# Order of two products in one PSUM accumulation: the second bias layer first, its correction products last

## Chip, core and metric

One Trainium2 chip, one of its cores, one launch. The metric is the device time of the launch in microseconds (us), lower is better. The engines are named as in the profile: PE is the matrix engine (PEld its weight loads), DVE the vector engine, ACT the scalar engine, POOL GpSimd, SP the engine that issues the DMAs.

## The reference, cut to what matters

Two layers of a deformable attention block run on x of shape (2, 128, 32, 32): 2 layers x 2 images, called four segments. Each has 8 heads of 16 channels, 1024 queries and 64 sampled keys. Most of the work is the position bias, a small network that is evaluated for each pair of query and key:

```python
pos = grid_q[:, :, None, :] - grid_kv[:, None, :, :]          # 1024 x 64 pairs, x and y, for each head
bias = jnp.sign(pos) * jnp.log1p(jnp.abs(pos))
bias = jax.nn.relu(bias @ cpb_w1 + cpb_b1)                    # 2 -> 32
bias = jax.nn.relu(bias @ cpb_w2 + cpb_b2)                    # 32 -> 32, the second layer
bias = (bias @ cpb_w3 + cpb_b3).reshape(b, GROUPS, H * W, Hd * Wd)   # 32 -> 1
sim = jnp.einsum('bhid,bhjd->bhij', qh, kh) + bias
attn = jax.nn.softmax(sim, axis=-1)
```

Before it come a grouped 1x1 product (q), a strided depthwise convolution, gelu, tanh, and a bilinear sampling of the image; after it the weighted sum of values, an output product with residual, and an MLP of 128 -> 512 -> 128 with residual.

## The kernel before, in words

The bias network is cut into 256 steps g: 4 segments x 4 pairs of heads (a pair of heads is a unit) x 16 steps. A step handles 16 keys and half of the queries (512): `ROWS` = 4 groups of 32 partitions and `CT` = 4 groups of 32 columns. Eight steps make a phase. In a step:

- DVE, `first_layer` (L565), writes h1, the first layer. It computes max(hx, hy') in one 128x2048 instruction, with hx = w1x*fx + b1 and hy' = -w1y*fy. Since relu(a + b) = max(a, -b) + b, what is stored lacks a term that depends on y alone. Three h1 buffers (`H1_BUFS`) let DVE run ahead; buffer g is free when pair 2(g-3)+1 is filled.
- PE, `layer2` (L753 to L774), sums in four PSUM banks (two "pairs" z(2g) and z(2g+1) of 1024 columns) the two parts of the second layer: the **correction products** (L766), sixteen matmuls of 32 partitions x 32 columns of bf16 weights `u_rows` against `fy`, which bring w2 times the missing term and the bias b2; and the **w2 products** (L771), sixteen matmuls of the same tile size in fp32, each of which the chip runs as two instructions. Ahead of the correction products of row groups 0 and 2 stands `turn`, the wait for the pair to be empty; between the two kinds stands the wait for h1.
- ACT, `relu2` (L426), reads each filled pair in one 128x1024 instruction and writes h2; the ring has three pairs (`RING`), so z(2g+1) of a step takes the pair that z(2g-2), the first pair of the step before, had.
- PE, `layer3` (L783), for the step before: four fp32 matmuls of 128 x 32 onto `scores`.

Other stages are put behind the step's own work by a table of slots (`BEFORE_SLOTS`, `AFTER_SLOTS`, `SOFTMAX_SLOTS`): PE runs `layer2(g)`, then `scores_start` (L795, once a phase), `layer3(g-1)`, then what the table names. In every phase slot 1 has the transposes (L873) and slot 2 the products that take off the maximum (L880). Slots 28 to 50 of a segment prepare the next one: among them on DVE `norm1`, `conv_products`, `hats` (L662) and `hat_products` (L668), on PE `q` (L818), `spread` (L842) and `sample` (L854). Slots 3 to 24 finish the segment before with `exp_sums`, `attend` (L891), `project` (L905), four `mlp_up` (L914) and `mlp_down` (L924). SP issues the loads of `fy` of a unit (`load_fy`) once the last z of the unit two before is filled, and `load_features` (hx, hy) when its h1 have been made; both serve a unit that starts 16 steps later.

Of the kernel before, what the change touches and what calls it, by code (L numbers as in the profile page):

```python
# [15 lines left out]
LAYERS, B, C, H, W = 2, 2, 128, 32, 32  # L16
# [18 lines left out]
ROWS = CT = 4  # L35
# [8 lines left out]
H1_BUFS = H2_BUFS = 3  # L44
# [128 lines left out]
def build(nc, x_in, consts, weights, x_out, features_dram, fy_dram, reciprocals_dram):  # L173
    with ExitStack() as ctx:
        def sb(name, shape, dt=F32):
            return ctx.enter_context(nc.sbuf_tensor(name, shape, dt))
# [4 lines left out]
        def sem(name):  # L181
            return ctx.enter_context(nc.semaphore(name))
# [35 lines left out]
        h1 = [sb(f"h1_{k}", [128, CT, HALF]) for k in range(H1_BUFS)]  # L218
# [5 lines left out]
        u_rows = [sb(f"u_rows{l}", [128, 128], BF16) for l in range(LAYERS)]  # L224
# [35 lines left out]
        h1_ready = sem("h1_ready")  # L260
# [15 lines left out]
        def w(l, name):  # L276
            a, b = COLS[name]
            return wts[l][:, a:b]
# [5 lines left out]
        def bank(h):  # L284
            return slice(HALF * h, HALF * (h + 1))

        def pair_of(stage, n):
            return pairs[PLACE[stage, n][0]]
# [461 lines left out]
        def _(pe):  # L750
            def layer2(g):


                unit, h, t = g // UNIT_STEPS, g // STRIDES % 2, g % STRIDES
                l = unit // PAIRS // B
                if g % UNIT_STEPS == 0:
                    pe.wait_ge(fy_loaded[unit % 2], 16 * ROWS * (unit // 2 + 1))
                    pe.wait_ge(u_ready, l + 1)
                z = [pair_of("z", 2 * g + r // 2)[:, bank(r % 2)] for r in range(ROWS)]
                key = [slice(32 * r, 32 * (r + 1)) for r in range(ROWS)]  # L760
                for r in range(ROWS):
                    if r % 2 == 0:
                        turn("z", 2 * g + r // 2)
                    y = fy[unit % 2][key[r], t, H // 2 * h:H // 2 * (h + 1)]
                    for c in range(CT):
                        pe.matmul(z[r][32 * c:32 * (c + 1)], u_rows[l][key[r], 32 * c:32 * (c + 1)],  # L766
                                  y.unsqueeze(2).broadcast_to([32, H // 2, W]), start=True, stop=False)
                pe.wait_ge(h1_ready, g + 1)
                for r in range(ROWS):
                    for c in range(CT):  # L770
                        ins = pe.matmul(z[r][32 * c:32 * (c + 1)], w(l, "w2")[key[r], key[r]], h1[g % H1_BUFS][key[r], c],  # L771
                                        start=False, stop=True)
                    if r % 2:
                        filled("z", 2 * g + r // 2, ins)  # L774

# [23 lines left out]
            def turn(stage, n):  # L799
                pair, _, before, _ = PLACE[stage, n]  # L800
                if before:
                    pe.wait_ge(pair_emptied[pair], before)

            def filled(stage, n, ins):
                ins.then_inc(pair_filled[PLACE[stage, n][0]], 1)
# [130 lines left out]
            for g in range(LAST_STEP + 1):  # L936
                if g == SEG_STEPS // 2:
                    pe.wait_ge(early_loaded[1], 16)
                    pe.wait_ge(late_loaded[1], 16)
                if g < ALL_STEPS:  # L940
                    layer2(g)
                if 1 <= g <= ALL_STEPS:
                    if g % STRIDES == 1:
                        scores_start(g // STRIDES)
                    layer3(g - 1)
                for name, n in PLAN["pe"].get(g, []):
                    stages[name](n)
# [92 lines left out]
```

## Time and profile before

| | |
|---|---|
| Time, three runs | 929.76 us median (927.41 to 930.80) |
| The profiled execution: its own time | 930.51 us |
| its span, first to last instruction | 928.7 us |
| mean granted PE clock | 0.97 of full speed |
| PE, DVE, ACT busy, share of the span | 91%, 77%, 69% |
| the 256 steps | 49.4 to 880 us of the span |
| a phase with nothing but its own stages | 22.41 us |

The profiled execution's own time is 1.8 us above its span, and 0.75 us above the median of the three runs. The span is one execution's; matmul durations in it are start to modelled end, and matmuls on different tiles overlap, so what a group costs PE is read from its start to the start of the group behind it.

### The profile page before, as it was taken

Reading aid. Unit: us, or ns where it says so; the run is one execution under the profiler, and the core shown is the slowest. Engines: PE = TensorE matmul, PEld = TensorE weight load, DVE = VectorE, ACT = ScalarE, POOL = GpSimd, SP = SyncE. Lnnn points to the kernel's source line nnn. Section 1 sums busy time; section 2 is a strip of 40 time slices with the busy share of each in tenths; the row PEclk is TensorE's granted clock in tenths of the full one; section 3 lists DMA queues with packets and bytes.
Section 4 is the critical chain, followed back from the end, with each engine's and each line's share of the span. In section 5 each row is a group of like instructions: output and inputs, shape, how many; then the busy total and the mean of one; then the engine's idle time right before and its main releaser. Section 6 shows DMA issues by size and latency. Waiting matters only on the chain.

```text
span 928.7 us, 34427 instructions
## 1 busy us (share of the span) xinstructions
PE 848.8 (91%) x15908; PEld 300.5 (32%) x15908; DVE 713.9 (77%) x472; ACT 639.5 (69%) x717; POOL 59.9 (6%) x40
## 2 busy tenths in 40 slices
PE   2179999989999999989999999999999999999936
PEld 1123323333333333323333333323333333333312
DVE  3678799898878659998878849989887749888411
ACT  1347768867777858877776857896777757777711
POOL 2200002120000002040000002040000000000000
PEclk9589999999999999999999999999999999999978
DMA  4210101011101101002011101002011101000010
GB/s 146 59 52 3 50 2 50 7 49 13 51 10 41 28 2 49 8 14 48 26 28 27 50 1 50 9 2 57 5 51 27 50 1 43 11 3 3 2 48 23
DMA packets 29535, 27.89 MB, mean 30 GB/s; under 512 B 22096, under 2 KB 24016, under 8 KB 29392
## 3 DMA queue, kind: packets, MB, share of 16 engines
q1 hardware_dynamic: 29392, 25.69, 10.6%
q8 instruction: 126, 2.06, 0.9%
q14 instruction: 17, 0.14, 0.1%
HBM read 23.05 MB, written 2.49 MB: 27 GB/s over the span
## 4 chain that ended last, share of the span: by engine, by line
PE 83%; DVE 8%; ACT 3%; DMA 3%; issue 2%; SPq 0%; POOL 0%; ACTq 0%; POOLq 0%; DVEq 0%
PE pair L771 29%; PE scores L783 24%; PE pair L766 9%; PE scores L795 3%; PE pair L914 3%; PE scores L880 3%; DVE h L565 3%; PE pair L924 3%; PE pair L873 2%; ACT h L426 2%; DVE big L668 2%; PE pair L891 1%; PE pair L905 1%; PE pair L818 1%; PE pair L854 1%
## 5 line engine op out<-in xcount | busy, mean ns | idle before, releaser
L426 ACT ACTIVATE h<-pair 128x1024 f32<-128x1024 f32 x512 | 496.5, 1022 | 201.9 <-PE pair L771 201.6
L565 DVE TENSOR_TENSOR h<-hx,hy 128x2048 f32<-128x2048 f32 x256 | 579.9, 2300 | 41.4 <-PE pair L771 41.1
L771 PE MATMUL pair<-h,wts 32*32 32x512 f32 x8192 | 346.6, 597 | 9.7 <-DVE h L565 9.7
L783 PE MATMUL scores<-h,wts 128*32 128x512 f32 x2048 | 273.6, 606 | 0.9 <-ACT h L426 0.9
L771 PEld LDWEIGHTS pair<-h,wts 32*32 32x32 f32 x8192 | 135.2, 103 | 29.3 <-DVE h L565 13.5
L766 PE MATMUL pair<-fy,u_rows 32*32 32x512 bf16 x4096 | 118.7, 386 | 27.4 <-DMA fy<-fy_dram 20.1
L783 PEld LDWEIGHTS scores<-h,wts 128*32 128x32 f32 x2048 | 43.6, 108 | 209.2 <-issue 208.4
L766 PEld LDWEIGHTS pair<-fy,u_rows 32*32 32x32 bf16 x4096 | 37.6, 88 | 196.7 <-issue 178.4
L691 DVE TENSOR_REDUCE neg_max<-pair 128x8 f32<-128x512 f32 x32 | 22.1, 691 | 70.3 <-PE pair L873 70.3
L306 POOL TENSOR_TENSOR conv_prod<-qpad,wts 128x288 f32<-128x288 f32 x16 | 21.6, 1379 | 440.3 <-ACT qpad L452 440.3
L406 POOL TENSOR_TENSOR big<-big,hat_x 128x512 f32<-128x512 f32 x16 | 35.5, 2248 | 119.0 <-DVE big L662 119.0
L719 DVE SCALAR_TENSOR_TENSOR x<-pair,wts,x 128x1024 f32<-128x1024 f32 x4 | 5.1, 1284 | 42.2 <-PE pair L924 42.2
L518 ACT ACTIVATE big<-pair,wts 128x1024 f32<-128x1024 f32 x16 | 17.8, 1114 | 27.7 <-PE pair L914 27.7
L880 PEld LDWEIGHTS scores<-const,neg_max 128*64 128x64 f32 x512 | 27.3, 136 | 27.0 <-issue 23.5
L880 PE MATMUL scores<-const,neg_max 128*64 128x128 f32 x512 | 35.0, 279 | 0.8 <-DVE neg_max L691 0.8
L914 PE MATMUL pair<-work,wts 128*128 128x512 f32 x64 | 32.7, 643 | 2.2 <-DVE work L713 2.2
L795 PE MATMUL scores<-qpad,keys_t 128*32 128x512 f32 x256 | 34.1, 605 | 0.0
L924 PE MATMUL pair<-big,wts 128*128 128x512 f32 x64 | 28.5, 598 | 1.3 <-ACT big L518 1.3
L512 ACT ACTIVATE probs<-scores,wts 128x512 f32<-128x512 f32 x32 | 22.0, 687 | 8.2 <-PE scores L880 8.0
L435 ACT ACTIVATE probs<-scores,wts 128x512 f32<-128x512 f32 x32 | 22.1, 692 | 1.3 <-PE scores L783 1.3
L873 PEld LDWEIGHTS pair<-const,probs 128*128 128x128 f32 x128 | 13.4, 140 | 27.7 <-issue 26.0
L873 PE MATMUL pair<-const,probs 128*128 128x128 f32 x128 | 21.0, 287 | 0.8 <-ACT probs L435 0.8
(87 smaller groups left out, 342.6 us busy)
## 6 DMA issues: line engine op xcount, KB each, us to landing
hx<-features_dram SPq DMA_DIRECT2D x64, 128.0 KB, 2.7
hy<-features_dram SPq DMA_DIRECT2D x64, 128.0 KB, 3.1
att_den<-reciprocals_dram SPq DMA_DIRECT2D x4, 512.0 KB
wts<-weights_dram SPq DMA_DIRECT2D x2, 960.0 KB, 8.5
fy_dram<-fy_part SPq DMA_DIRECT2D x96, 8.0 KB, 1.5
x<-x_dram SPq DMA_DIRECT2D x2, 512.0 KB, 5.9
fy<-fy_dram SPq DMA_DIRECT2D x64, 12.0 KB
out_dram<-x SPq DMA_DIRECT2D x2, 512.0 KB, 4.9
```

Source lines behind the costliest of these rows:

```text
L406: pool.tensor_tensor(bilinear[:, k], hat_y[:, k], hat_x[:], ALU.mult).then_inc(bilinear_ready[0], 1)
L426: emptied("z", 2 * g + j, act.activation(h2[g % H2_BUFS][:, 2 * j:2 * (j + 1)].rearrange("p r n -> p (r n)"), pair_of("z", 2 * g + j)[:], ...
L435: act.activation(probs[:, unit % PAIRS, bank(h)], scores[phase % 2][:], ACT.Identity, bias=w(seg // B, "b3"))\
L565: dve.tensor_tensor(h1[g % H1_BUFS][:].rearrange("p c (y x) -> p c y x", x=W), hx[unit % 2][:, :, t].unsqueeze(2).broadcast_to([128, CT, H ...
L766: pe.matmul(z[r][32 * c:32 * (c + 1)], u_rows[l][key[r], 32 * c:32 * (c + 1)], y.unsqueeze(2).broadcast_to([32, H // 2, W]), start=True, s ...
L771: ins = pe.matmul(z[r][32 * c:32 * (c + 1)], w(l, "w2")[key[r], key[r]], h1[g % H1_BUFS][key[r], c], start=False, stop=True)
L783: ins = pe.matmul(scores[phase % 2][32 * r:32 * (r + 1)], w(l, "w3")[:, 32 * t:32 * (t + 1)], h2[g % H2_BUFS][:, r], start=False, stop=t = ...
L795: pe.matmul(scores[phase % 2][k], keys_t[seg % 2][:, u, k], qpad[seg % 2][:, 1 + H // 2 * h:1 + H // 2 * (h + 1), 1:W + 1], start=True, st ...
L873: ins = pe.transpose(pair_of("scores_t", phase)[:, s], probs[:, unit % PAIRS, bank(h)][:, s], cst("ident"))
L880: ins = pe.matmul(scores[phase % 2][NKV * n:NKV * (n + 1), 128 * k:128 * (k + 1)], neg_max[phase % 2][:, 2 * k + n:2 * k + n + 1].broadcas ...
L914: ins = pe.matmul(pair_of("mlp_up", n)[:, bank(h)], w(seg // B, "mlp_w1")[:, 128 * c:128 * (c + 1)], xn2[:, bank(h)], start=True, stop=True)
L924: ins = pe.matmul(pair_of("mlp_down", seg)[:, bank(h)], w(seg // B, "mlp_w2")[:, 128 * c:128 * (c + 1)], mlp_h[:, c, bank(h)], start=c == ...
```

## The change

In `layer2` the two kinds of product change places. The w2 products come first and start each PSUM accumulation; the correction products come second, end it, and the last one of each pair signals that the pair is filled. `turn` (the pair is empty) and the wait for h1 now both stand ahead of the w2 products; the waits for `fy` and `u_rows`, once a unit, stand between the two kinds. The instructions, their number, shapes and data are the same.

```diff
                 unit, h, t = g // UNIT_STEPS, g // STRIDES % 2, g % STRIDES
                 l = unit // PAIRS // B
+                z = [pair_of("z", 2 * g + r // 2)[:, bank(r % 2)] for r in range(ROWS)]
+                key = [slice(32 * r, 32 * (r + 1)) for r in range(ROWS)]
+                pe.wait_ge(h1_ready, g + 1)
+                for r in range(ROWS):
+                    if r % 2 == 0:
+                        turn("z", 2 * g + r // 2)
+                    for c in range(CT):
+                        pe.matmul(z[r][32 * c:32 * (c + 1)], w(l, "w2")[key[r], key[r]], h1[g % H1_BUFS][key[r], c],
+                                  start=True, stop=False)
                 if g % UNIT_STEPS == 0:
                     pe.wait_ge(fy_loaded[unit % 2], 16 * ROWS * (unit // 2 + 1))
                     pe.wait_ge(u_ready, l + 1)
-                z = [pair_of("z", 2 * g + r // 2)[:, bank(r % 2)] for r in range(ROWS)]
-                key = [slice(32 * r, 32 * (r + 1)) for r in range(ROWS)]
                 for r in range(ROWS):
-                    if r % 2 == 0:
-                        turn("z", 2 * g + r // 2)
                     y = fy[unit % 2][key[r], t, H // 2 * h:H // 2 * (h + 1)]
                     for c in range(CT):
-                        pe.matmul(z[r][32 * c:32 * (c + 1)], u_rows[l][key[r], 32 * c:32 * (c + 1)],
-                                  y.unsqueeze(2).broadcast_to([32, H // 2, W]), start=True, stop=False)
-                pe.wait_ge(h1_ready, g + 1)
-                for r in range(ROWS):
-                    for c in range(CT):
-                        ins = pe.matmul(z[r][32 * c:32 * (c + 1)], w(l, "w2")[key[r], key[r]], h1[g % H1_BUFS][key[r], c],
-                                        start=False, stop=True)
+                        ins = pe.matmul(z[r][32 * c:32 * (c + 1)], u_rows[l][key[r], 32 * c:32 * (c + 1)],
+                                        y.unsqueeze(2).broadcast_to([32, H // 2, W]), start=False, stop=True)
                     if r % 2:
                         filled("z", 2 * g + r // 2, ins)
```

## Rows read from the trace of the kernel before

**Rows 1.** The page: busy time, and the chain that ended last.

```profile
PE 848.8 (91%) x15908; PEld 300.5 (32%) x15908; DVE 713.9 (77%) x472; ACT 639.5 (69%) x717; POOL 59.9 (6%) x40
PE 83%; DVE 8%; ACT 3%; DMA 3%; issue 2%; SPq 0%; POOL 0%; ACTq 0%; POOLq 0%; DVEq 0%
```

**Rows 2.** Timeline of PE in a plain phase: start, us, group.

```profile
812.15 0.43 PE L766 MATMUL pair<-fy,u_rows 32*32 32x512 bf16 x16
812.37 1.34 PE L771 MATMUL pair<-h,wts 32*32 32x512 f32 x32
813.64 1.07 PE L783 MATMUL scores<-h,wts 128*32 128x512 f32 x8
814.64 0.43 PE L766 MATMUL pair<-fy,u_rows 32*32 32x512 bf16 x16
814.87 1.34 PE L771 MATMUL pair<-h,wts 32*32 32x512 f32 x32
...
816.04 1.94 ACT L426 ACTIVATE h<-pair 128x1024 f32<-128x1024 f32 x2
```

**Rows 3.** Busy time in four phases of eight steps: length, PE, PEld, DVE, ACT, POOL, clock, DMA.

```profile
812.15:834.56 22.41, 22.41 (x480) 7.57 (x477) 19.57 (x12) 16.75 (x19) 0.00 (x0) 1.00 0.01 2
...
339.12:364.70 25.58, 25.58 (x493) 9.14 (x490) 24.44 (x17) 19.99 (x22) 5.90 (x4) 1.00 0.17 44
364.70:391.34 26.64, 24.75 (x500) 9.68 (x496) 25.70 (x25) 23.65 (x30) 0.00 (x0) 1.00 0.05 9
391.34:419.79 28.45, 25.70 (x544) 9.06 (x541) 26.16 (x18) 22.77 (x27) 9.45 (x4) 1.00 0.09 24
```

**Rows 4.** The waits of the whole span: us in total, times, longest.

```profile
ACT h L426 <- PE pair L771: 201.6, 197, 17.4
DVE h L565 <- PE pair L771: 41.1, 55, 2.1
PE pair L771 <- DVE h L565: 9.7, 12, 1.6
```

**Rows 5.** L771 alone in short stretches: matmuls, loads that ran or had run (x).

```profile
814.86:814.96 0.10, 0.09 (x8) 0.10 (x9) 1.00 0.00 0
...
57.82:57.84 0.02, 0.02 (x16) 0.02 (x28) 1.00 0.00 0
...
58.21:58.22 0.01, 0.01 (x24) 0.00 (x0) 1.00 0.00 0
```

**Rows 6.** Timeline: loads issued behind the correction products' start, stretch cut at 841.2 us.

```profile
840.99 0.43 PE L766 MATMUL pair<-fy,u_rows 32*32 32x512 bf16 x16
841.05 0.18 PEld L771 LDWEIGHTS pair<-h,wts 32*32 32x32 f32 x9
```

**Rows 7.** Timeline, the steps at 57.7 us and at 199.1 us.

```profile
57.71 1.15 PE L771 MATMUL pair<-h,wts 32*32 32x512 f32 x32 [1.12 <-DVE h L565]
58.79 1.07 PE L795 MATMUL scores<-qpad,keys_t 128*32 128x512 f32 x8
...
58.91 1.02 ACT L426 ACTIVATE h<-pair 128x1024 f32<-128x1024 f32 x1 [1.20 <-PE pair L771]
...
199.11 1.15 PE L771 MATMUL pair<-h,wts 32*32 32x512 f32 x32 [0.73 <-DVE h L565]
```

**Rows 8.** The line L766: duration ns min/median/max of its matmuls.

```profile
L766 PE MATMUL pair<-fy,u_rows x4096: 384/385/605, 49.4 to 876.9; 32*32 32x512 bf16 x196
```

**Rows 9.** Timeline of the start: the wait for fy, then for the first h1.

```profile
49.43 0.66 PE L766 MATMUL pair<-fy,u_rows 32*32 32x512 bf16 x16 [20.08 <-DMA fy<-fy_dram]
50.54 2.02 PE L771 MATMUL pair<-h,wts 32*32 32x512 f32 x32 [0.45 <-DVE h L565]
```

**Rows 10.** Behind a wait for h1: timeline; then two stretches, clock eighth column.

```profile
118.60 2.02 PE L771 MATMUL pair<-h,wts 32*32 32x512 f32 x32 [1.65 <-DVE h L565]
...
118.60:122.20 3.60, 3.60 (x40) 0.49 (x40) 3.60 (x2) 1.63 (x2) 0.00 (x0) 0.53 0.00 0
...
173.40:176.80 3.40, 3.40 (x58) 0.92 (x56) 2.29 (x1) 3.01 (x4) 0.00 (x0) 0.51 0.00 0
```

## Prediction

> **What bounds the kernel now.** I read the page first: PE is busy 91% of the span and the chain that ended last lies 83% on it [rows 1], so what the change does to PE's own sequence comes first. Then the timeline of PE in a phase that has no other work than its own. There a step takes 814.64 - 812.15 = 2.49 us, without a gap: 0.22 us from the correction products to the w2 products, 1.27 us from these to layer 3, and 1.00 us from layer 3 to the next step [rows 2]. PE is the bound in such a phase; DVE is busy 19.57 of 22.41 us [rows 3]. The waits say the same: PE waited for h1 only 12 times, 9.7 us in all, while ACT waited for PE 197 times and DVE 55 times [rows 4]. The exception is the three phases in which DVE prepares the next segment: DVE busy is 24.44 of 25.58, 25.70 of 26.64 and 26.16 of 28.45 us [rows 3]. Three of the four segments have such a stretch.
>
> **The change, step by step.** No instruction, byte or DMA is added. What moves is where the w2 products stand, and the trace of before happens to show them both ways.
>
> 1. *w2 products behind correction products (now).* The reader should see that the 1.27 us are not what sixteen tiles need. The first instruction of each fp32 product starts on eight tiles together; the other eight have not started 0.1 us later, and nine loads are in (the first of [rows 5]). In the next view too exactly nine w2 loads get in while the correction products hold the tiles [rows 6]. The second half of the tiles starts late, and everything behind it on those tiles too.
>
> 2. *w2 products on tiles that are free (the other order's case).* At 57.71 us PE had waited for h1, the correction products were long through, and the same 32 instructions took 58.79 - 57.71 = 1.08 us to the start of the next group [rows 7]. All sixteen first instructions ran within 0.12 us (the second of [rows 5]). So 1.27 - 1.08 = 0.19 us a step is a cost of standing behind the bf16 products. After the change they stand behind layer 3, whose tiles have another size; a group behind such a switch starts with no load done ahead (L795 stands so too and starts at once [rows 7]). I take it as the free case.
>
> 3. *Correction products behind w2 products (new).* The trace has no row of it. Lower bound: their loads go in while the second fp32 instructions run, and they add only what they now take up to the next start, 0.22 us [rows 2]: 1.08 + 0.22 = 1.30 us against 1.49 now. Upper bound: no load gets in until the w2 matmuls have ended (1.15 us after their start [rows 7]), then a load of about 0.1 us (0.18 us for nine overlapped loads in rows 6 is the nearest row), then the products (0.43 us to their end, of which some 0.1 overlaps the next group [rows 2]): about 1.15 + 0.1 + 0.3 = 1.55, that is 0.06 us more than now. I take the lower one, because in rows 6 loads do go in under running matmuls of the same tiles, from the moment these have started.
> A rule bears on this. The Trainium skill ("TensorE: Matmul & The Clock Gate", Part 3) says that a weight load overlaps matmuls in flight only when the row group differs; by it the upper bound would hold and the step would not shrink. The trace disagrees with the rule as worded: the w2 loads start 0.06 us after the correction matmuls of the same row groups, which take 0.385 us each [rows 6, 8]. That page's Part 2 adds the background weight buffer, which would fit.
>
> 4. *The ACT loop, which is next late.* z(2g+1) takes the pair that relu reads first in the step before, and the wait for it now stands ahead of the w2 products of row group 2 instead of ahead of the short products. Counted from the w2 products' start: eight second instructions have started at 0.50 (58.21 [rows 5]), one lasts about 0.43 on its tile (the step from first to second, 57.71 to 58.16), so the last correction product of row group 1 starts at 0.93; it lasts 0.385 [rows 8]; ACT starts some 0.12 behind an end (58.91 against 58.21 + 0.59) and takes 1.02 [rows 7]: 2.46, and a wake-up of 0.05 (estimate) makes 2.51. Row group 2 wants the pair 0.06 after the start of the next w2 products, so nothing stalls in a step of 2.45 us or more; with 1.30 + 1.00 = 2.30 us a step it comes 0.15 late. A late step is longer, which gives the next one its time back, so steps would alternate between 2.30 and 2.45: 0.075 lost on the average. Now the same count leaves the pair empty at 0.22 + 1.17 + 1.02 + 0.05 = 2.46 after the step's start, some 0.06 before it is wanted at 2.49 + 0.03 [rows 2, 7], so that the loop hardly shows.
>
> 5. *The h1 loop.* h1 is wanted 0.22 us earlier in a step and given back 0.22 us later. With three buffers and 2.3 to 2.5 us a step DVE keeps some 3 us in hand, and in a plain phase 22.41 - 19.57 = 2.8 us of it are idle [rows 3]. No cost there. In the three stretches DVE has nothing to spare, and what PE saves PE then waits.
>
> 6. *Waits for fy and u.* The waits on fy move behind the w2 products. Only the first is ever long (20.08 us), and there h1 comes later still, at 50.54 [rows 9]. Now the correction products of step 0 run in that wait; after, they stand behind the w2 products at half clock: +0.4 us. The loads of SP stay where they were, a unit ahead; what releases them (the last z) comes at the same place of the step.
>
> **The sum.** 256 steps. 72 lie in the three stretches, 184 outside; of these 3 already start free (of the 12 waits nine lie in the stretches, three in each like the one at 199.11 us, and three before and outside them [rows 4, 7]), so 181 x 0.19 = 34.4 us. Of the 23 phases outside, six steps in eight follow a step with no other stage, 138, less 8 in each of three segments that follow a stage of slots 3 to 22: 114 x 0.075 = 8.6 us back to the ACT loop. The stretches: a phase can't be shorter than DVE's busy time plus the 0.95 us that the tightest has (26.64 - 25.70), which leaves 0.2 us in one phase of a stretch and little more in the first segment: 2 us in all. The start: -0.4. Together 34.4 - 8.6 + 2 - 0.4 = 27.4 us. The profiled execution took 930.51 us, hence 903.1; it is 0.75 above the median of the runs, which I leave in the rounding: 903 us.
>
> **Rivals.**
> - *No gate by ACT.* If the pair is free in time after all, 8.6 us come back, and if the stretches gain half of 63 x 0.19 instead of 2 us, 4 more: about 890 us. For it: ACT is only 75% busy in a phase [rows 3]. Against: the count of step 4.
> - *The loads of the correction products don't go in early* (the upper bound of step 3). Then a step has 2.55 instead of 2.49 us: 184 x 0.06 = +11 us, 941 us. It decides from the point where the correction products start more than about 1.18 us after the w2 products (0.99 by my count). For it: no row shows bf16 behind fp32 on the same tiles. Against: rows 6. With only the streaming waited for, the start would be at 1.08 and the step 2.4: no ACT gate, 915 us.
> - *DVE is the bound everywhere.* If DVE's lead fails at each unit's `hidden_terms` and each phase's `score_max`, a phase would stay near 22 instead of about 21.3: some 0.4 x 23 = 9 us gained, 920 us. Against: 2.8 us of idle DVE a phase.
> - *The clock.* Behind a wait of PE for h1 the clock was granted at 0.53 for 3.60 us, the 1.2 GHz level [rows 10], some 1.8 us lost; a second such dip at 173.4 us lies in the first stretch, in which PE also waits. Longer waits in the stretches may add one or two for each: +4 to +10 us on top of any case.
>
> **How the numbers follow.** Chances: forecast with its own range 896 to 913: 0.5; no ACT gate, 884 to 896: 0.14; a gain cut to a few us by DVE or by partly hidden loads, 913 to 925: 0.18; no change: 0.06; loads not hidden, or dips that eat the gain: 0.12. Below 884 I leave 0.04 of the second, above 926 the last two, so the range 884 to 926 leaves out about 0.2. 0.5% of the time is 4.6 us, about what a measurement of this kernel tells from no change. Faster by more than that: 0.82; within: 0.06; slower: 0.12.
>
> **What the profile of the changed kernel would show.** In a plain phase the w2 matmuls take 1.08 to 1.3 us of start to last end with all sixteen tiles started in 0.12 us, the correction products start some 0.9 to 1.0 us after them, and layer 3 1.30 us after them (step 3 wrong if 1.4 or more). Steps alternate near 2.30 and 2.45, and the second half of the w2 products shows a wait for L426 (step 4 wrong if steps are all 2.30). A plain phase lasts 21.2 to 21.4 us. The stretches keep their length within 1 us, with more waits for L565. More than two mid-run stretches of low clock would spoil the sum. PE's busy time drops by about what the span does, DVE's and ACT's stay.

## The result, and the profile after

| | before | after |
|---|---|---|
| Time, median of 13 runs each on the same chip | 930.49 us (927.41 to 931.77) | 934.37 us (930.23 to 938.0) |
| Ratio, with its 95% interval | | 1.0044 (1.003 to 1.0057) |
| Profiled execution: own time, span | 930.51, 928.7 us | 934.73, 932.9 us |
| Mean granted PE clock | 0.97 | 0.967 |

The change made the kernel 3.9 us slower, within the half per cent that was called no change; 903 us had been forecast, with a range to 926. In the kernel after, L763 are the w2 products and L771 the correction products; layer 3 is still L783.

The page of the kernel after and the longest wait for PE in it, against [rows 1, 4] (a wait: us in total, times, longest):

```profile
PE 850.2 (91%) x15908; PEld 314.9 (34%) x15908; DVE 715.4 (77%) x472; ACT 639.9 (69%) x717; POOL 59.9 (6%) x40
```

```profile
ACT h L426 <- PE pair L771: 210.2, 194, 17.9
```

PE is busy 91% of the span as before, ACT waits for it as often, and the counts of instructions are equal. The answer lies inside a step. Timeline of the kernel after, a plain step (start, us, group, idle before), against [rows 2]:

```profile
828.81 1.21 PE L763 MATMUL pair<-h,wts 32*32 32x512 f32 x32
829.26 0.28 PEld L771 LDWEIGHTS pair<-fy,u_rows 32*32 32x32 bf16 x2 [0.15 <-issue]
829.69 0.68 PE L771 MATMUL pair<-fy,u_rows 32*32 32x512 bf16 x16
829.88 0.20 PEld L771 LDWEIGHTS pair<-fy,u_rows 32*32 32x32 bf16 x14 [0.34 <-issue]
...
830.30 1.06 PE L783 MATMUL scores<-h,wts 128*32 128x512 f32 x8
...
831.30 0.66 PE L763 MATMUL pair<-h,wts 32*32 32x512 f32 x8
```

From w2 to the correction products it is 829.69 - 828.81 = 0.88 us, from these to layer 3 0.61, from layer 3 to the next step 1.00: 2.49 us, as before. The w2 products now have the free case's early second halves, as forecast. But the correction products, which took 0.22 us when they stood first, take 0.61 now. Two of their loads go in ahead; the other fourteen come from 829.88 on, 0.19 us after the first product has started. L771 alone shows it (us, PE busy (x), PEld busy (x), clock):

```profile
829.75:829.76 0.01, 0.01 (x1) 0.00 (x0) 1.00 0.00 0
829.98:829.99 0.01, 0.01 (x15) 0.01 (x12) 1.00 0.00 0
```

One correction product is under way 0.06 us after the first, and 0.29 us after it there are fifteen. In [rows 5] it was the w2 products that had only eight tiles going while their ninth load was in. The lag has moved from one set to the other: 1.49 us from a step's start to layer 3, as before.

Plain phases are equal to 0.01 us (842.76 - 820.36 = 22.40, [rows 3] 22.41). The 3.9 to 4.2 us lie elsewhere, and the starts of L795, once a phase, show where. The kernel after is behind by 1.78 us at the first, 2.55 at the second, 1.27 at the fourth (130.06 against 128.79), 1.98 after the first stretch (212.32 against 210.34), 2.61 after the second (427.46 against 424.85), 4.31 after the third and 4.20 at the last. Three things make up these steps.

*The start*, timelines against [rows 7, 9]:

```profile
49.76 2.02 PE L763 MATMUL pair<-h,wts 32*32 32x512 f32 x32 [21.30 <-issue]
52.33 3.42 PE L854 MATMUL pair<-big,image_t 128*32 128x128 f32 x64
...
58.38 1.74 PE L763 MATMUL pair<-h,wts 32*32 32x512 f32 x32 [1.49 <-DVE h L565]
60.57 1.08 PE L795 MATMUL scores<-qpad,keys_t 128*32 128x512 f32 x4
```

Before, the correction products of steps 0 and 1 ran while PE waited for h1. Now PE idles there, and they come behind. In step 0 it is 2.57 us from w2 to the sampling products L854 (49.76 to 52.33), against 1.95 before (50.54 to 52.49); h1 came 0.78 us earlier in this execution, which hid these 0.62 us. But the clock stayed at the 1.2 GHz level until 55.4 us (0.50 from 53.9 to 55.4, where the kernel before had 1.00), and from L854 to the products behind it, L864, it took 3.85 us against 3.02. That is why step 1 starts 0.67 us later. In step 1 it takes 2.19 us from w2 to L795 against 1.08. Behind an awaited h1 at full clock it is 1.50 (see below), so 0.42 us of this comes with the order, and the other 0.69 with the 1.2 GHz level, which begins at 58.8 us. Together 0.67 + 1.11 = 1.78.

*The stretches.* A late h1, the kernel after, against the 199.11 us of [rows 7]:

```profile
200.69 1.15 PE L763 MATMUL pair<-h,wts 32*32 32x512 f32 x32 [0.85 <-DVE h L565]
201.57 0.68 PE L771 MATMUL pair<-fy,u_rows 32*32 32x512 bf16 x16
202.19 1.06 PE L783 MATMUL scores<-h,wts 128*32 128x512 f32 x8
```

Behind an awaited h1 stand 1.50 us instead of 1.08. Phases inside the stretches (length, PE, PEld, DVE, ACT, POOL, clock). The kernel before, the second phase of the first and of the second stretch:

```profile
182.91:210.34 27.43, 25.02 (x544) 9.01 (x541) 26.40 (x18) 20.36 (x25) 8.85 (x4) 1.00 0.17 42
396.35:424.85 28.50, 26.03 (x544) 9.10 (x541) 27.48 (x18) 20.60 (x25) 8.85 (x4) 1.00 0.16 41
```

The kernel after, the second phase of the first stretch, the first phase of the third, and a short piece at low clock:

```profile
184.29:212.32 28.03, 25.12 (x548) 9.68 (x540) 27.17 (x18) 20.41 (x24) 9.05 (x4) 1.00 0.18 42
585.74:614.56 28.82, 26.70 (x504) 10.01 (x496) 25.25 (x26) 25.29 (x33) 0.40 (x1) 0.94 0.04 7
389.90:393.30 3.40, 3.40 (x52) 0.73 (x42) 2.29 (x1) 3.16 (x4) 0.00 (x0) 0.50 0.00 0
```

28.03 - 27.43 = 0.60 us are lost in such a phase at full clock, and as much in the third stretch (28.05 against 27.43). In the second the kernel after is 0.47 us faster (28.03 against 28.50), but only because this execution of the kernel before lost 1.07 us in a single step: from w2 to layer 3 it took 2.34 us (420.02 to 422.36) instead of 1.27. No run says why; e7, with the same order there, has 27.42 us in this phase.

*The clock.* The last row is a stretch at the 1.2 GHz level. Between 56 and 880 us the kernel after has three more, at 58.8, 174.9 (clock 0.50 each) and 604.9 us (0.51). Before there were two, at 118.6 and 173.4 us [rows 10]. The phase at 585.74 holds the one at 604.9: 28.82 us, against 27.66 for the same phase before at clock 1.00. The missing one at 118.6 us gives 1.2 us back (the lag falls from 2.49 to 1.27).

Added up over the phases (an estimate from the differences above), the order itself costs some 2.2 us, 0.4 at the start and 0.6 in each stretch. Differences in clock cost some 3 us more, and the late step of the kernel before takes 1.1 off.

### The profile page after: what moved, and what is told of

It reads as the page before. It is cut to its first block, busy times and chain, and to the rows that moved or that the text cites. A ratio compares the mean times of both kernels' runs of the same rounds, so it can differ in the third digit from the quotient of the medians.

```text
span 932.9 us, 34682 instructions
## 1 busy us (share of the span) xinstructions
PE 850.2 (91%) x15908; PEld 314.9 (34%) x15908; DVE 715.4 (77%) x472; ACT 639.9 (69%) x717; POOL 59.9 (6%) x40
## 3 DMA queue, kind: packets, MB, share of 16 engines
HBM read 23.05 MB, written 2.49 MB: 27 GB/s over the span
## 4 chain that ended last, share of the span: by engine, by line
PE 85%; DVE 7%; issue 4%; DMA 2%; ACT 1%; POOL 0%; SPq 0%; ACTq 0%; POOLq 0%; DVEq 0%
PE pair L763 29%; PE scores L783 25%; PE pair L771 10%; PE scores L795 4%; PE pair L914 3%; PE scores L880 3%; PE pair L924 3%; DVE h L565 3%; PE pair L873 2%; PE pair L891 1%; PE pair L842 1%; PE pair L818 1%; PE pair L905 1%; PE pair L854 1%; DVE big L668 1%
## 5 line engine op out<-in xcount | busy, mean ns | idle before, releaser
L763 PE MATMUL pair<-h,wts 32*32 32x512 f32 x8192 | 313.8, 607 | 40.0 <-issue 21.3
L783 PE MATMUL scores<-h,wts 128*32 128x512 f32 x2048 | 274.5, 608 | 1.1 <-ACT h L426 1.1
L771 PE MATMUL pair<-fy,u_rows 32*32 32x512 bf16 x4096 | 180.0, 383 | 0.0
L771 PEld LDWEIGHTS pair<-fy,u_rows 32*32 32x32 bf16 x4096 | 96.2, 88 | 156.2 <-issue 120.4
L763 PEld LDWEIGHTS pair<-h,wts 32*32 32x32 f32 x8192 | 71.8, 103 | 212.5 <-issue 142.0
L783 PEld LDWEIGHTS scores<-h,wts 128*32 128x32 f32 x2048 | 43.6, 108 | 76.0 <-issue 76.0
L306 POOL TENSOR_TENSOR conv_prod<-qpad,wts 128x288 f32<-128x288 f32 x16 | 21.6, 1381 | 441.3 <-ACT qpad L452 441.3
L795 PE MATMUL scores<-qpad,keys_t 128*32 128x512 f32 x256 | 34.9, 618 | 0.0
```

The costliest lines, as they stand in the source:

```text
L771: ins = pe.matmul(z[r][32 * c:32 * (c + 1)], u_rows[l][key[r], 32 * c:32 * (c + 1)], y.unsqueeze(2).broadcast_to([32, H // 2, W]), start=F ...
L783: ins = pe.matmul(scores[phase % 2][32 * r:32 * (r + 1)], w(l, "w3")[:, 32 * t:32 * (t + 1)], h2[g % H2_BUFS][:, r], start=False, stop=t = ...
L795: pe.matmul(scores[phase % 2][k], keys_t[seg % 2][:, u, k], qpad[seg % 2][:, 1 + H // 2 * h:1 + H // 2 * (h + 1), 1:W + 1], start=True, st ...
```

## Experiments

The kernels below have the product order as a list, `ORDER(g)`, for each step: `w` is the four fp32 w2 products of a row group, `f` its four 32x32 correction products, `F` one 32x128 correction product for the whole row group in place of the four. The other lines of the edits, which only make this list work, are left out. In the timelines w2 products are L789 to L791, narrow correction products L792 to L794, wide ones L786 to L788, layer 3 L812 to L814.

**e1: w2 products alone.** Is the free case 1.08 us in every step, and does ACT gate a shorter one?

```diff
-    w0 w1 w2 w3 f0 f1 f2 f3
+    w0 w1 w2 w3                  # the waits for fy and u stay
```

> The sixteen correction products are left out (their waits are kept); the w2 products stand alone between two groups of 128x32 tiles. Three theories of the 0.19 us that the forecast lost. A, queue: behind a group that waits for busy tiles of the same tile size, PE has only part of the rest at hand and the rest starts about 0.185 us late; a change of tile size (a drain) cures it. B, type: going from bf16 to fp32 on a tile, or back, costs 0.19 us. C, throughput: sixteen tiles simply need 1.49 us for both kinds, of which 0.22 are the corrections'. A and B: the w2 products take 1.08 us from their start to layer 3's, all sixteen tiles started within 0.12 us; PE then needs 2.08 us a step, so DVE (2.27) or the ACT loop sets steps of 2.25 to 2.35 us and the time is about 870 to 885 us. C: 1.27 us from w2 to layer 3 and steps of 2.27 us at least, with the eight late tiles still there.

Measured: 864.34 us (before 929.77). Timeline of e1:

```profile
747.73 1.16 PE L789 MATMUL pair<-h,wts 32*32 32x512 f32 x32
748.82 1.06 PE L812 MATMUL scores<-h,wts 128*32 128x512 f32 x8
749.82 1.28 PE L789 MATMUL pair<-h,wts 32*32 32x512 f32 x32
751.02 1.07 PE L812 MATMUL scores<-h,wts 128*32 128x512 f32 x8
```

1.09 us to layer 3, then 1.20: steps alternate between 2.09 and 2.20. The time is below the 870 to 885 us expected, and so are the steps (2.25 to 2.35). Steps 2 and 4 of the prediction hold as mechanisms. The free case is there in a plain step. In every other step the second pair is late: in the step at 749.82 us its first w2 product starts at 750.00, 0.05 us behind the end of ACT's relu of the first pair of the step before (749.95). The correction set costs 65 us in the original order, 0.25 us a step, though its instructions are among the shortest.

**e2 and e3: the corrections as four wide products, first or last.** If the lag belongs to a second set on the same busy 32x32 tiles, a change of tile size should remove it.

```diff
-    w0 w1 w2 w3 f0 f1 f2 f3
+    F0 F1 F2 F3 w0 w1 w2 w3      # e2
+    w0 w1 w2 w3 F0 F1 F2 F3      # e3
```

> The correction products come first again, but as four matmuls of 32 partitions x 128 columns (u_rows of a row group in one weight load) instead of sixteen of 32x32; the same sums. The tile size now changes between them and the w2 products. A: corrections 0.31 us to the w2 start, then w2 in 1.08 us on free tiles: 1.39 us instead of 1.49; the rest of the step 1.00. Without another limit 2.39 us a step and about 908 us; if the wait of the second pair for ACT's relu of the step before binds at about 2.45 us, only about 920 us. B: w2 behind a change of type still takes 1.27 us: 1.58 us for both, step 2.57 us, about 948 us. C: 1.49 to 1.58, no gain.

> The changed order with the corrections as four matmuls of 32x128. A: w2 starts free (1.08 us to the corrections' start, drain included), corrections 0.31 us: 1.39 us; the gate by ACT then shows, since the pair is filled later (about 1.6 us after the w2 start): steps of 2.39 to 2.6, on average near 2.45 to 2.49; time 915 to 930 us, not better than the wide corrections first. B: 1.58 us for both, about 950 us.

Measured: e2 936.73 us, ratio 1.0072 (1.0057 to 1.0087); e3 930.42 us, 0.9999 (0.9987 to 1.0012). Timeline of e2, a step behind other stages, then a plain one:

```profile
822.31 0.40 PE L786 MATMUL pair<-fy,u_rows 32*128 32x512 bf16 x4
822.63 1.14 PE L789 MATMUL pair<-h,wts 32*32 32x512 f32 x32
...
828.15 0.57 PE L786 MATMUL pair<-fy,u_rows 32*128 32x512 bf16 x4
828.66 1.14 PE L789 MATMUL pair<-h,wts 32*32 32x512 f32 x32
829.73 1.08 PE L812 MATMUL scores<-h,wts 128*32 128x512 f32 x8
830.74 0.39 PE L786 MATMUL pair<-fy,u_rows 32*128 32x512 bf16 x2
```

Timeline of e3, the same two kinds of step:

```profile
821.97 1.14 PE L789 MATMUL pair<-h,wts 32*32 32x512 f32 x32
823.05 0.40 PE L786 MATMUL pair<-fy,u_rows 32*128 32x512 bf16 x4
823.37 1.06 PE L812 MATMUL scores<-h,wts 128*32 128x512 f32 x8
824.37 1.28 PE L789 MATMUL pair<-h,wts 32*32 32x512 f32 x32
825.58 0.40 PE L786 MATMUL pair<-fy,u_rows 32*128 32x512 bf16 x4
825.90 0.64 PE L812 MATMUL scores<-h,wts 128*32 128x512 f32 x4
```

Where nothing else holds it, the wide set costs 0.32 us in either place and w2 keeps its 1.07 or 1.08 (821.97 to 823.05): 1.39 or 1.40 us to layer 3 instead of 1.49, and the lag is gone. A plain step is 2.59 us in e2 (830.74 - 828.15) and 2.53 in e3 (825.90 - 823.37) all the same. In e2 the wide set is stretched to 0.51, in e3 the w2 set to 1.21: both are held by the pair that ACT has not emptied (in e3 the relu ends at 824.50 and the second pair's w2 products start at 824.55). What the tiles give is taken by the next loop. So the part of theory A on the tiles came as expected, but its times did not, 908 to 920 us for e2 and 915 to 930 for e3, since the wait for ACT bound at 2.59 and 2.53 us instead of near 2.45.

**e4: the kinds mixed**, so that only eight products of a second set follow at a time.

```diff
-    w0 w1 w2 w3 f0 f1 f2 f3
+    f0 f1 w2 w3 w0 w1 f2 f3
```

> Same instructions as before, another order: corrections of row groups 0 and 1, w2 of 2 and 3, w2 of 0 and 1, corrections of 2 and 3. A: the w2 products of 2 and 3 start at once on free tiles, those of 0 and 1 are the only ones to wait (0.21 us), and a group of eight that waits can be followed late by at most the eight corrections: 1.25 to 1.45 us for all instead of 1.49, time 905 to 930 us. B: each tile still changes type once within the step: 1.49, no change. C: no change.

Measured: 947.21 us, ratio 1.0189 (1.0172 to 1.0206). In its timeline the step at 817.01 us has 0.22 us to w2 (817.23), 0.86 from there to the second half of the corrections (818.09) and 0.56 to layer 3 (818.65), 1.64 us in all; in the next, w2 comes after 0.07 us and layer 3 after 1.49 (819.65 to 821.14). At best the mixed order equals the others, and it adds 0.15 us in other steps. There the w2 products of the second pair come first, and that pair is empty late: they start 0.14 us behind the end of ACT's relu in both steps (817.09 and 819.58; not tested by itself). The expectation of 905 to 930 us under theory A was missed, and this order doesn't hide the lag either.

**e5: the w2 products twice.** Is it the meeting of bf16 and fp32, or any second set on the same tiles?

```diff
-    w0 w1 w2 w3 f0 f1 f2 f3
+    w0 w1 w2 w3 w0 w1 w2 w3
```

> The correction products are replaced by the w2 products a second time (another sum): fp32 behind fp32 on the same sixteen tiles. Queue theory: the second set is late like any set behind busy tiles, both together take 0.86 + 1.04 + the late start of 0.19, about 2.1 us to the next group, and its first instructions start in two lots 0.185 us apart. Type theory: no change of type, so both take 1.08 + 0.86 = 1.94 us, all started within 0.12 us. Time about 930 + 256 x 0.5 = 1060 us at most, not the point.

Measured: 1114.68 us. Timeline of e5:

```profile
901.36 2.35 PE L789 MATMUL pair<-h,wts 32*32 32x512 f32 x64
903.64 0.64 PE L812 MATMUL scores<-h,wts 128*32 128x512 f32 x4
```

And its line L789 alone in two short stretches:

```profile
902.26:902.42 0.16, 0.16 (x17) 0.09 (x1) 1.00 0.00 0
902.50:902.51 0.01, 0.01 (x7) 0.01 (x8) 1.00 0.00 0
```

2.28 us for both sets, where two times the time to the next start (0.88, and 1.08 at the end) would be 1.96. In the 0.16 us from 902.26 on, one single load goes in; only then do the others follow. The second set's first product starts at 902.24 and the next at 902.44, the same 0.19 us; the other products then start 17 ns apart instead of 7, which is the rest of the 0.32 us (2.1 us had been expected for both sets). One type, and a first product that is alone for 0.19 us: a change of type is out as its cause.

**e6: the correction products twice, behind w2.** Is the 0.61 us a fee of the set, or one paid once?

```diff
-    w0 w1 w2 w3 f0 f1 f2 f3
+    w0 w1 w2 w3 f0 f1 f2 f3 f0 f1 f2 f3
```

> The changed order with the correction products twice (another sum): w2, corrections, corrections. The first set should start 0.88 us after w2 with a spread of 0.30 us as in the changed kernel. The second is bf16 behind bf16. Queue theory: the second set is late as well or is issued at the pace of 8 ns a tile that the first has: it adds 0.2 to 0.4 us. Type theory: it adds 0.21 us, started within 0.05 us of its turn, since the type stays.

Measured: 980.97 us. Timeline of e6:

```profile
856.24 1.21 PE L789 MATMUL pair<-h,wts 32*32 32x512 f32 x32
857.12 0.90 PE L792 MATMUL pair<-fy,u_rows 32*32 32x512 bf16 x32
857.31 0.33 PEld L792 LDWEIGHTS pair<-fy,u_rows 32*32 32x32 bf16 x30 [0.34 <-issue]
857.95 0.64 PE L812 MATMUL scores<-h,wts 128*32 128x512 f32 x4
```

Both sets together take 0.83 us; the second adds 0.22, the price that the corrections had in the original order. So sixteen bf16 products behind bf16 products cost 0.22 us even on busy tiles: behind the first two, the other thirty loads go in without a stop, and no product of the second set starts alone. That is what the type theory had expected of this run, and the low end of what the queue theory had. And the 0.39 us more is paid once, where the first of them meets the w2 products: 0.20 of it is the rest of w2's own 1.08 us (they begin at 0.88), and 0.19 is lag.

**e7: the original order where the change loses.** Steps 0 and 1 and slots 24 to 51 of the first three segments have the original order, all others the changed one.

```diff
+    if g < 2 or g < SEG_STEPS * (SEGS - 1) and 24 <= g % SEG_STEPS < 52:
+        return f0 f1 f2 f3 w0 w1 w2 w3
     w0 w1 w2 w3 f0 f1 f2 f3
```

> The changed order everywhere but in steps 0 and 1 and in slots 24 to 51 of the first three segments, where the order of before is kept (86 of 256 steps). My account now: in plain phases both orders take 22.41 us, and all of the loss is in these places: the corrections of step 0 and 1 no longer run while PE waits for h1 at the 1.2 GHz level, and behind a wait of 2.2 us for h1 near 390 and 605 us the clock drops where it did not. So this kernel should be within 0.15% of the one before, about 930 us, with low clock near 174 us at most. Rival: the loss comes from the order in all steps (a later fill of the pairs for ACT, h1 given back later); then two thirds of it stay, 933 us.

Measured: 931.55 us, ratio 1.0021 (1.0008 to 1.0033). Long stretches of e7, against 638.30 to 860.97 us of before (222.67 us long, x4362) and 860.97 to the end (67.73 us, PE 44.70 of it, clock 0.87):

```profile
638.56:861.18 222.62, 222.62 (x4361) 80.06 (x4356) 178.82 (x95) 163.11 (x177) 0.00 (x0) 1.00 0.09 21
861.18:931.10 69.92, 46.88 (x477) 17.59 (x468) 15.48 (x11) 23.45 (x25) 0.00 (x0) 0.85 0.07 24
```

The start and the stretches have their old lengths (183.02 to 210.45 us is 27.43 again), and at 861 us e7 is 0.2 us behind the kernel before instead of 4.2. The medians give back less: e7 is 2.0 us above the kernel before (931.55 against 929.58), where the change was 3.9. That lies between the two accounts (at most 0.15%, or two thirds of the loss, which is 0.29%), and an interval from 0.08% to 0.33% doesn't tell them apart. What this execution still loses, 2.2 us, lies in the last 70 us, most of it behind the last step, at a clock of 0.85 against 0.87; whether the others of its runs lose theirs there too, no profile shows. e7 also has a stretch at the 1.2 GHz level (clock 0.50 from 388.2 to 391.4 us), in steps with the original order, and is 1.3 us behind at the end of that phase. In the next the distance falls back to 0.2, but only because the kernel before has its late step there. So part of e7's closeness at 861 us is luck, and the place of such a stretch does not hang on the order of the products around it alone.

**e8: wide corrections where ACT has time.** From e2 and e3: wide products first, but only in the steps behind which another stage gives ACT its time.

```diff
+    if PLAN["pe"].get(g):
+        return F0 F1 F2 F3 w0 w1 w2 w3
     f0 f1 f2 f3 w0 w1 w2 w3
```

> The order of before, with the corrections as four matmuls of 32x128 in those steps behind which PE has another stage to run (some 110 of 256), as sixteen of 32x32 elsewhere. If the tile drain saves 0.10 us a step and only the wait for ACT's relu of the step before took it back in the kernel with wide corrections everywhere, then the stage behind gives ACT the time, and 110 x 0.10 less those in which DVE sets the pace is 6 to 10 us: 920 to 925 us. Rival: the later fill of the first pair delays ACT in the next step as well, and nothing or less than 2 us is gained.

Measured: 924.01 us, ratio 0.9932 (0.9915 to 0.9949): faster than both kernels. Timeline of e8:

```profile
790.19 0.39 PE L788 MATMUL pair<-fy,u_rows 32*128 32x512 bf16 x4
790.52 1.14 PE L791 MATMUL pair<-h,wts 32*32 32x512 f32 x32
791.59 1.08 PE L814 MATMUL scores<-h,wts 128*32 128x512 f32 x8
```

1.40 us to layer 3 in a wide step; a narrow one, at 796.12 us, has 1.50. 100 steps are wide (400 of these products), so 0.09 to 0.10 each gives 9 to 10 us, less what the stretches keep; 5.6 us were measured, within the 920 to 925 us expected. The clock has a part in it in both directions: this execution is 2.1 us behind at the second L795 (81.71 against 79.61 us), with a low stretch from 58.9 us on, and has none at 118.6 or 173.4 us. From 638.30 us on (633.74 in e8), where both run at clock 1.00, the same nine phases take 220.75 us instead of 222.67, so the gain is not the clock's alone. A plain phase, with two such steps, takes 22.25 us (832.24 to 854.49) instead of 22.41.

**e10 and e11: a shorter relu.** relu reads one bank of each pair, which takes ACT out of the loop; e10 has the order of e2, e11 that of the change.

```diff
-    activation(h2[.., both banks], pair[.., 0:1024], Relu)
+    activation(h2[.., one bank],   pair[.., 0:512],  Relu)   # the other bank of h2 is zeroed once
```

> The kernel with corrections first as four matmuls of 32x128, and ACT's relu over only the first 512 of the 1024 columns of each pair (the other half of h2 stays zero, so half of the second layer's output is left out). With the whole relu the plain steps took 2.59 us although PE's own parts sum to 1.40 + 1.00. If the wait for the relu of the step before is what holds them, they fall to 2.39 to 2.42 us now and the late start of the second pair's corrections (0.19 us) is gone; a plain phase then takes 21.6 us or less. Rival: the drains or DVE hold them, then they stay above 2.5.

> The changed kernel with the same shorter relu (half of the second layer's output left out). Plain steps have been 2.49 us. If the late start behind busy tiles alone sets them, they stay at 2.49 us, 1.49 of it from the w2 products to layer 3, with the corrections' first matmul 0.88 us behind w2 and the rest 0.185 us later. If ACT's loop has a part in the 2.49 us, they fall below 2.45.

Measured: e10 905.15 us, e11 922.57 us (before 930.27). Timeline of e10:

```profile
801.22 0.39 PE L787 MATMUL pair<-fy,u_rows 32*128 32x512 bf16 x4
...
803.63 0.39 PE L787 MATMUL pair<-fy,u_rows 32*128 32x512 bf16 x4
```

Timeline of e11:

```profile
799.22 1.16 PE L790 MATMUL pair<-h,wts 32*32 32x512 f32 x32
800.10 0.69 PE L793 MATMUL pair<-fy,u_rows 32*32 32x512 bf16 x16
800.71 1.07 PE L813 MATMUL scores<-h,wts 128*32 128x512 f32 x8
801.71 0.73 PE L790 MATMUL pair<-h,wts 32*32 32x512 f32 x16
```

The plain step of the wide order falls from 2.59 to 2.41 us: the 0.18 us was the wait for ACT. That of the changed order stays at 2.49: ACT was not what held it, the lag was. e11 is all the same 11.8 us below the changed kernel (one run, 922.57 against 934.37). Its plain phases take the same 22.41 us; what shrinks is the first phase of each stretch, where ACT has other work too (25.79 us in the third, against 28.82, in part since it has no low clock there). e10's plain phase takes 21.75 us, where 21.6 or less was expected.

**e12: one row group of corrections behind w2.** Does the lag grow with the number of products, or is it fixed?

```diff
-    w0 w1 w2 w3 f0 f1 f2 f3
+    w0 w1 w2 w3 f3
```

> The changed kernel with only the four corrections of row group 3 (those of groups 0 to 2 are left out). Is the late start a constant of each change from one set to the next on busy tiles, or does it grow with the number of matmuls? Constant: first correction about 0.98 us after w2 (its tile's second half started at 0.53 to 0.61), the others 0.185 us later, and layer 3 about 0.30 us after the last: 1.45 to 1.50 us, nearly as much as with all sixteen. Growing: 1.25 to 1.35 us.

Measured: 913.29 us. Timeline of e12:

```profile
799.66 1.16 PE L789 MATMUL pair<-h,wts 32*32 32x512 f32 x32
800.62 0.50 PE L792 MATMUL pair<-fy,u_rows 32*32 32x512 bf16 x4
801.06 0.64 PE L824 MATMUL scores<-qpad,keys_t 128*32 128x512 f32 x4
```

0.96 us to the correction products, 0.44 from these on: 1.40 us, between what the two theories gave. Four products cost 0.32 us (1.40 - 1.08), sixteen 0.41 (1.49 - 1.08). The first product starts 0.96 us after w2 instead of 0.88 and is alone for 0.10 us instead of 0.19. Both simple rules, a fixed fee and one in proportion, miss it; how the size of the lag comes about stays open.

## Why the prediction was wrong

**Step 3 failed.** It took the lower bound, 0.22 us for correction products behind w2 and layer 3 at 1.30 us; they cost 0.41 and layer 3 came at 1.49. Its own mark, "wrong if 1.4 or more", was passed. With the step at 2.49 us, neither the 34.4 us of gain nor the 8.6 us back to the ACT loop was there. The argument from [rows 6] was that loads do go in under running matmuls of the same tiles. They do, but the rows say nine of sixteen, and the ninth tile then starts late: the rows that showed the lag were read as proof that there would be none. In the new order it is worse, two instead of nine. The upper bound, 1.55 us, was within 0.06 of the truth, though by another way: it had the first product start after 1.18 us, and it started after 0.88. For a cost bounded by 1.30 and 1.55, the observed one of the same kind (0.19 us for the second of two sets) was the nearest row, and adding it gives 1.08 + 0.22 + 0.19 = 1.49.

The Trainium skill ("TensorE: Matmul & The Clock Gate", Part 3) has a weight load overlap matmuls in flight only when the row group differs. The trace agrees in the main and not in the letter: fourteen of the sixteen loads wait here, but two go in at 829.26 us, under w2 products of their own row group. As a forecast of this change it did better than the reading that set it aside.

**Step 1 had the right size and the wrong owner.** The 0.19 us is not the price of standing behind bf16 products. The set that comes second on the same 32x32 tiles pays it in all three pairings with fp32 products that were run: fp32 behind bf16 (the kernel before), bf16 behind fp32 (the kernel after), fp32 behind fp32 (e5). bf16 behind bf16 did not pay it, but was seen only once, as the third set of e6; whether one of the two sets has to be fp32 is not shown. Neither of the orders tried (the change, e4) took the lag away, and a set of another tile size does (e2, e3, e8). The Trainium skill ("TensorEngine Tiling (Array Packing)", Key Properties) says that a change of tiling mode drains the engine. The 0.32 us that four wide products hold up w2 or layer 3, nearly the 0.385 us that each lasts, would fit. Here such a switch is the cheaper of the two.

**Step 2 was right**: 1.08 to 1.09 us on free tiles (e1), and 0.88 to the next set in the kernel after.

**Step 4 was right as a mechanism and out of reach of the change.** Steps of 2.09 and 2.20 us alternate in e1; the wide orders stop at 2.53 and 2.59; with the short relu 2.41 is reached. In the changed kernel the plain step stayed at 2.49. (The count took 0.43 us for 57.71 to 58.16, which is 0.45; that moves the gate by 0.02 us.) Of the rival "no gate by ACT" nothing was left.

**Step 5 and the stretches**: no cost in plain phases, as said; in the stretches 2 us were forecast as gain, and at full clock about 0.6 us was lost in each. Since the step did not shrink, only the other side of the move was left: work that had filled the waits for h1 came to stand behind them. **Step 6** had the place right and 0.4 us for it. Step 0 does pay 0.62 us, hidden by an earlier h1. The 1.8 us seen are another sum: step 1 pays 0.42 us too, and the clock is low for longer, which the step had left out. **The clock** rival's dips came, four against two, at about 1.2 us each and not 1.8. e7 took the order back in these places and lost 0.2 us up to 861 us instead of 4.2; by the medians 2.0 instead of 3.9. Of the changed kernel's thirteen runs the fastest (930.23 us) has the highest clock, 0.972, and the slowest (938.0 us) the lowest, 0.961. No run varied the clock by itself, so how much of the 4 us is its doing beyond the rows above is not separated, and whether the order brings the dips on is not shown.

The range was too narrow at the top: its upper end left out both the case of no change and the bound of step 3, each worked out beforehand, while rows 5 and 6 showed the cost that decided.

## What to carry to other kernels

Where a set of small matmuls follows another on the same busy tiles and one of the two is fp32, expect the set that comes second to start late; here swapping the two moved the lag and didn't remove it, while fewer and wider products, with another tile size, did. Before counting a saving on PE, look up which loop is next (here ACT's pair, which held the wide orders at 2.53 and 2.59 us a step) and spend the cheaper form only where that loop has slack. Work that fills a wait is free there and costs its full time once it stands behind the wait.

## What the runs showed of the hardware

- On busy 32x32 tiles the second set starts in two lots. Under bf16 products nine loads get in ahead and eight fp32 products start together, the ninth 0.19 us after the first (814.87 and 815.05 us, kernel before). Under fp32 products two loads get in, the first product runs alone, and the rest follow 0.19 us after it (829.69 and 829.88 us, kernel after; the same in e5). Behind bf16 products a bf16 set shows no such stop (e6). With only four products behind w2 it is 0.44 us to the next group (e12). Why the counts differ, no run here tells.
- Four 32x128 products cost their neighbours 0.32 us, sixteen 32x32 ones 0.22 us standing first plus 0.19 for the lag of the set behind (1.27 - 1.08).
- At 388.44 us of the kernel after PE had waited 2.12 us, and the clock was at 0.50 from 389.9 on; the kernel before waited 1.89 us at the same place (386.36) and kept 1.00, and e7 waited the same 1.89 us in the same order (386.54) and was at 0.50 from 388.2 on. What decides it is open.
